# Graph-network kernel: where TensorE transposes the edge rows in the first two slots of a pass

## The reference

```python
def _sage_conv(x, src, dst, W_l, b_l, W_r):
    msgs = x[src]
    agg = segment_sum(msgs, dst, num_segments=N_NODES)
    deg = segment_sum(ones, dst, num_segments=N_NODES)
    mean = agg / maximum(deg, 1.0)[:, None]
    return mean @ W_l + b_l + x @ W_r
h = relu(_sage_conv(x, src, dst, W1_l, b1, W1_r))
h = relu(_sage_conv(h, src, dst, W2_l, b2, W2_r))
out = layernorm(x + (h @ W3 + b3))          # over the 256 features, eps 1e-5
```

## Time and profile before

| | us |
|---|---|
| median of 3 runs | 2946.12 |
| lowest and highest | 2945.32, 2947.18 |
| the profiled execution, its own time | 2948.13 |
| its span, first to last instruction | 2946.3 |
| TensorE busy in it | 2844.9 (97%) |
| VectorE busy | 2284.1 (78%) |
| ScalarE busy | 1962.4 (67%) |
| GpSimd busy | 1855.1 (63%) |

### The profile page before, as it was taken

The page is one execution under the profiler, slowest core; times in us unless marked ns, Lnnn a source line. Parts: engine busy times, 40 slices in busy tenths (PEclk is TensorE's granted clock), DMA queues, the critical chain, the costliest instruction groups (busy, mean ns, idle before and its releaser), DMA issues. The chain is left out here.

```text
span 2946.3 us, 54699 instructions
## 1 busy us (share of the span) xinstructions
PE 2844.9 (97%) x18457; PEld 2578.4 (88%) x18457; DVE 2284.1 (78%) x4001; ACT 1962.4 (67%) x2992; POOL 1855.1 (63%) x1732
## 2 busy tenths in 40 slices
PE   5999999999999999999999999999999989989996
PEld 4999999999999999999999999999999978878885
DVE  5787777778787777878787777878787779889896
ACT  3676766767676766767676766767676646555654
POOL 5665665656665665656565665656565557777776
PEclk9999999999999999999999999999999999999998
DMA  4444544545444544445444544445444466656663
GB/s 132 151 157 146 168 152 149 164 146 167 146 158 145 167 153 150 163 146 167 146 159 145 166 153 150 162 146 167 146 159 146 136 215 234 233 215 223 231 227 140
DMA packets 253121, 488.25 MB, mean 166 GB/s; under 512 B 37615, under 2 KB 165206, under 8 KB 253090
## 3 DMA queue, kind: packets, MB, share of 16 engines
q1 hardware_dynamic: 202498, 387.58, 39.1%
q0 software_dynamic: 50176, 99.91, 10.4%
q10 hardware_dynamic: 416, 0.40, 0.0%
HBM read 284.67 MB, written 206.22 MB: 167 GB/s over the span
## 5 line engine op out<-in xcount | busy, mean ns | idle before, releaser
L486 ACT ACTIVATE pair<-pair,bias 128x512 f32<-128x512 f32 x784 | 513.6, 660 | 671.3 <-PE pair L860 656.4
L391 POOL TENSOR_TENSOR xb<-xn,b_row 128x1024 f32<-128x1024 f32 x196 | 469.2, 2394 | 549.1 <-DVE y L670 548.9
L648 DVE TENSOR_TENSOR h_lo<-pair,h_hi 128x1024 fp32r<-128x1024 f32 x392 | 476.9, 1217 | 280.2 <-ACT h_hi L488 279.5
L871 PE MATMUL pair<-w_hi,h_hi 128*128 128x256 f32 x1960 | 562.2, 287 | 4.9 <-DVE h_lo L648 3.1
L871 PE MATMUL pair<-w_lo,h_hi 128*128 128x256 f32 x1960 | 554.3, 283 | 0.0
L871 PE MATMUL pair<-w_hi,h_lo 128*128 128x256 f32 x1960 | 554.2, 283 | 0.0
L345 POOL DMA_INDIRECT xe<-in_x_dram,e_stage x392 | 406.9, 1038 | 176.5 <-issue 97.7
L499 ACT ACTIVATE o<-y,nb,rs 128x256 f32<-128x256 f32 x784 | 408.2, 597 | 3.5 <-DVE nb L701 3.5
L488 ACT CAST h_hi<-pair 128x1024 fp32r<-128x1024 f32 x392 | 397.5, 1014 | 12.4
L860 PE MATMUL pair<-xt_hi,w_hi 128*128 128x512 f32 x980 | 401.2, 409 | 3.6 <-DVE run L722 2.1
L860 PE MATMUL pair<-xt_lo,w_hi 128*128 128x512 f32 x980 | 385.3, 393 | 0.0
(11 more groups left out here) (124 smaller groups left out, 6237.9 us busy)
## 6 DMA issues: line engine op xcount, KB each, us to landing
xn<-in_x_dram SPq DMA_DIRECT2D x196, 512.0 KB, 4.2
out_dram<-o SPq DMA_DIRECT2D x196, 512.0 KB, 2.9
seg<-seg_tab SPq DMA_DIRECT2D x74, 512.0 KB, 5.1
xdb_tab<-xdb SPq DMA_DIRECT2D x49, 512.0 KB, 4.9
h_tab<-src_h SPq DMA_DIRECT2D x49, 512.0 KB
h_tab<-dst_h SPq DMA_DIRECT2D x49, 512.0 KB, 6.3
xn<-h_tab SPq DMA_DIRECT2D x49, 512.0 KB, 5.1
xb<-xdb_tab SPq DMA_DIRECT2D x49, 512.0 KB, 4.2
```

Of the source, the lines that this page charges most:

```text
L391: nc.gpsimd.tensor_tensor(xb[:, b], xn[:, u], b3_row[:, :].unsqueeze(1).to_broadcast([P, S, D]), ALU.add).then_inc(xb_ok, 1)
L486: nc.scalar.activation(ps[:, k], ps[:, k], ACT.Relu, bias=bias[:, n, k:k + 1]).then_inc(hf_ok[n], 1)
L648: nc.vector.tensor_tensor(h_lo[:, h], ps[:, :, :], h_hi[:, h].bitcast(f32), ALU.subtract).then_inc(hlo_ok[n], 1)
L871: ins = nc.tensor.matmul(ps[:, s // 2, s % 2 * D:(s % 2 + 1) * D], a[:, k, s * P:(s + 1) * P], wx[:, w, k], start=first, stop=end)
```

## The change

On TensorE's queue the transposes of the edge rows in slots 0 and 1, with the wait for `y_ok` in front of them, move from behind layer 1 to directly behind the transposes of x. The code for them is split off `edges` as `turn_ends`. In slots 2 and 3 nothing moves. No instruction is added or taken away, and the other engines' programs are the same.

```diff
-            def edges(i, u, ps):
-                xs, xd = (xe_hi[:, 0], xe_lo[:, 0]), (xe_hi[:, 1], xe_lo[:, 1])
+            def turn_ends(i, u, ps):
                 if u == 0:
                     pe.wait_ge(xs_in, 16 * S * (i + 1))
                     for k in range(K):
...
                     pe.wait_ge(xd_in, 16 * S * (i + 1))
                     for k in range(K):
                         turn(ps, xe[:, 1], k).then_inc(xd_ps, 1)
+
+            def edges(i, u, ps):
+                xs, xd = (xe_hi[:, 0], xe_lo[:, 0]), (xe_hi[:, 1], xe_lo[:, 1])
                 if u == 2:
...
                         turn_rows(i + (u + 2) // U, (u + 2) % U, pair[u])
+                    if u < 2:
+                        after(pe, y_ok, g - 1)
+                        turn_ends(i, u, pair[(u + 2) % 4])
                     if not (last and u == 3):
                         pe.wait_ge(xlo_ok, g + 2)
                         edges_left(i, u)
                         first_layer((u + 1) % 2, pair[(u + 1) % 4])
-                    after(pe, y_ok, g - 1)
-                    edges(i, u, pair[(u + 2) % 4])
+                    if u >= 2:
+                        after(pe, y_ok, g - 1)
+                        edges(i, u, pair[(u + 2) % 4])
```

## The result

The changed kernel takes 3013.7 us (median of 4 runs, 3010.66 to 3014.62) against 2946.65 us for the kernel before (median of 4 runs, 2945.32 to 2948.86). The ratio is 1.0225 with a 95% interval of 1.0207 to 1.0243: 67 us slower. The forecast was 3017 us, range 3004 to 3034.

A forecast was written before the change was run, and what follows sets the result against it. TensorE, busy 97% of the span, was taken to bound the kernel. A new slot 1 wait of 1.48 us in 48 passes gave 71.0 us, added to the 2946.12 median: 3017 us, range 3004 to 3034.

The forecast's parts named there:

- TensorE sets the loop, a merge saves nothing: Main loop: TensorE busy 2259.95 of 2263.00 us; merging two transpose groups gives nothing, to within 0.01 us.
- a gain of 8 us: Other bound for merging transposes: 0.08 us per merge, 98 merges over the 49 passes; the forecast took 0.
- The residual moves on by 0.88 us: Slot 0: layer 1 ends 0.88 us later, and VectorE's tight chain moves the residual's end from 1237.97 to 1238.85.
- Slot 1's wait: TensorE waits for y_ok behind slot 1's x transposes: 1.28 us, plus 0.15 release and 0.05 restart, 1.48 per pass.
- No other wait, nothing paid back: Rest of the pass: the 1.48 us stay; slot 1's layer 3 has 0.8 us in hand, later residual waits over 2.
- the 0.15 taken from the first pass: Release from VectorE's scan end to TensorE's start, read at 51.56 to 51.71; bounds 0.03 and 0.26 us.
- the list of waits: Other waits checked: slot 1's layer 3, the residuals for slots 2 and 0, gathered rows, GpSimd's addition; no stall expected.
- The first pass cancels: First pass: no y_ok wait in slot 1; later scans and earlier destination transposes about cancel, 0 within 1.5 us.
- The clock: New 1.43 us idle stretch per pass: no clock loss expected; rival, a fall costing 1.7 us each, chance 0.10.
- Rival 3 (part of the wait given back): VectorE's chain moves by less than 0.88 us or layer 1 starts earlier: at most 12 us less, 3005; chance 0.10.
- Rival 2: No wait at slot 1's y_ok, shorter chain or older semaphore group: 0 to 8 us off, 2938 to 2946; chance 0.05.

The follow-up runs named there:

- slot 0 alone: Changed kernel with only slot 0's edge transposes and wait moved, slot 1 in the old order: 2988.35 us, ratio 1.0137 to the kernel before.
- the two longer waits in the same place: Changed kernel with one extra VectorE instruction ahead of slot 0's scans: a 480-column addition, 3036.41 us (ratio 1.0315), or a 480-column scan, 3132.57 us (1.0609).
- the kernel with the addition: Changed kernel with one more VectorE addition of 480 columns, result unread, ahead of slot 0's scans: 3036.41 us, ratio 1.0315 to the kernel before.

## Why the prediction was right, and where it was not

- **TensorE sets the loop, a merge saves nothing.** Held: 20.25 against 20.23 us for the two slots without waits. Counting from a group's start to the second matmul behind it, instead of taking the gap of 0.31 us behind a group as a loss, was what kept a gain of 8 us out of the sum.
- **The residual moves on by 0.88 us.** Held: 12.29 us after the slot's start, 12.27 by the working.
- **Slot 1's wait.** Predicted 1.28 + 0.15 + 0.05 = 1.48 us. Measured 1.41 for the pass: between the residual's end and TensorE's start were 0.05 us, not the 0.15 taken from the first pass, and from the edge transposes on the slot takes 9.32 us where the parts give 9.25, so the start without weights loaded ahead cost 0.07 and not 0.05. The release is the term that was too large. 48 x 0.07 = 3.4 us of the 4 by which the rise (67 us by the medians) lay below the 71 forecast.
- **No other wait, nothing paid back.** Held for this kernel: slots 2 and 3 keep their time, layer 3 of slot 1 had 0.73 us in hand (0.8 predicted). But the list of waits left out the scans that layer 1 asks for in slot 1, and it did not see that they and layer 3 have room only because TensorE is already late. For the change itself this did not matter, which is luck and not working; for slot 0 alone it made the expectation wrong by 40 us.
- **The first pass cancels.** Not quite: it ended 1.9 us earlier, outside the 1.5 allowed either way. The wait for the scans shrank from 2.15 to 1.61 us, and the fall of the clock behind it, which the working had not looked at, was absent too.
- **The clock.** Forecast as no loss at this length with 0.10 for a loss. Held. Of the two longer waits in the same place 1.73 us cost nothing in any pass and 2.21 us cost a fall in 42 of 48, so in that place the 1.16 us were clear of it. The Trainium skill ("TensorE: Matmul & The Clock Gate", "Part 4: PE-mode transpose") says that transposes do not count for the clock as matmuls do. That the clock fell behind 2.21 us of waiting between two groups of transposes fits it. So does the wait of 3.06 us with matmuls on both sides in the kernel before, behind which the clock stayed up. But this is one wait per run, and the 3.09 us behind sixteen transposes left the clock up as well. The rule is not shown here, as no two runs differ only in what stands beside the wait.
- **Rival 3 (part of the wait given back)** did not happen: ScalarE's idle time before the second ReLU grew from 0.25 to 0.72 us, and VectorE's idle by the full 0.89. **Rival 2** did not either, the count of `y_ok` was the one worked out.

## What to carry to other kernels

On an engine that is full, moving an instruction costs nothing by itself and gains nothing by itself; look at what comes later (whose chain hangs on the work it was moved ahead of) and at what is asked for earlier (each wait that travels with it), and subtract both from the time in hand. Do that for every result of the late queue that the next stage asks for, since a wait that is found first hides the others. A wait that gets longer is paid one for one only until the clock joins in: here up to 1.73 us, and no longer at 2.21.

## What the runs showed of the hardware

- Eight fp32 transposes of 128x128 cost TensorE 0.88 us of its time, 0.11 each, alone or behind eight others, though each is recorded with 0.27 us.
- In the loop, TensorE's record starts 0.05 us after the end of the VectorE instruction that releases it (1221.80 to 1221.85, and 1212.79 to 1212.84), not the 0.15 of the first pass.
- The granted clock stayed at its upper level with a wait of 1.73 us in each pass and fell to the lower one in 42 of 48 passes with 2.21 us; the fall that was read cost 1.58 us. Single waits of 3.06 us (between matmuls, kernel before) and 3.09 us (behind sixteen transposes, first pass of the kernel with the addition) did not lower it.
